# Four small transformer layers on one NeuronCore: the second layer's attention in two score orientations on 32-row tiles

## The chip, the core and the metric

The kernel runs on one core of a Trainium2 chip. The metric is device microseconds of one launch, from input in HBM to output in HBM. TensorE is PE here (its weight loads PEld), VectorE is DVE, ScalarE is ACT, GpSimd is POOL. All four work at once, each on its own list of instructions, and wait for one another by semaphores; PE writes into 8 PSUM banks of 128 partitions x 512 f32, from which ACT and DVE read.

## What is computed

x is [4, 256, 128] in f32: four batches of 256 tokens with 128 features. Four layers follow one another, all conditioned on `cond_1024` [4, 128]: an attention block with 16 heads of 64 and an MLP; the block below; a gated recurrence with rounded weights; a linear attention. The change touches only the attention of the second layer:

```python
nx = _ada_rmsnorm(x, time_emb, w_norm1, t1_w1, t1_b1, t1_w2, t1_b2)
q = (nx @ wq + bq).reshape(b, s, 16, 8)      # k and v likewise
q = q * c + _rotate_half(q) * si             # k likewise
scores = einsum('bshd,bthd->bhst', q, k) / sqrt(8)
probs = softmax(scores, axis=-1)
attn = einsum('bhst,bthd->bshd', probs, v).reshape(b, s, 128)
x = x + attn @ wo + bo
```

Per batch there are 16 heads of width 8 and scores of 256 x 256. The third layer also needs 768 parameters per batch from a chain of five small products on 4 rows (its "ada" chain: wa0, wa1, wa2, wa3, a norm, wa4), which doesn't depend on x.

## The kernel before

All 64 (batch, head) pairs n of the second layer go through one loop, written out by hand on each engine; the order of the instructions on an engine is the order of that engine's program.

**Split numbers.** q and k are kept in the format fp32r, each as a rounded part and the remainder (`high_parts` on ACT, L594, `low_parts` on DVE, L1594). A head of width 8 so takes 32 rows (high and low, twice), and four heads share a 128-row tile: `qaT` and `kaT` hold them, made by transposes on PE (L1041 to L1050).

**Prologue.** For all 8 token tiles: the QKV product (PE, L1027 to L1037), bias and rotary embedding (DVE, L1602 to L1617), high and low parts, transposes, copies into `qaT` and `kaT` (ACT, L601 to L609). PE waits for all 16 copies before the loop (L1051). As the score matmul runs over all 128 rows, the keys of a head are copied alone into a tile that is zero elsewhere (`kaM`, `masked_key`); the zeros come from a memset on POOL (L402).

**Loop** (PE L1096, ACT L655, DVE L1693). For head i:
- PE `scores` (L837): two matmuls, queries of 128 tokens against 256 keys, into bank i % 2.
- DVE `top` (L1437): the largest score of each query, negated.
- ACT `core_exp` (L501): exp with that bias, two instructions, each with an accumulator read for the sum; then the key copy of head i + 16.
- PE `turn` (L846), two heads behind: four 128 x 128 transposes of the probabilities.
- DVE `take` (L1443): copy to SBUF.
- PE `values` (L854), three heads behind: for both query tiles two f32 matmuls with 96 columns of v streamed against the turned probabilities as weights.
- DVE `normalise` (L1449), once for four heads.

**Woven in.** `weave(i)` on ACT (L626), PE (L1074) and DVE (L1640) puts one step of the ada chain behind head i, by the table `WEAVE` and the offsets USE to RESULT (L278 to L282). POOL rounds the weights of the third layer meanwhile. A Silu in this chain makes ACT load its table, and then exp's again. The outputs of the first two batches (`turn_outputs`, `outputs`, `attention_out`) stand at steps 61 to 66, those of the other two behind the loop (L1126 to L1129).

**The first attention** (L907 to L943), which the prediction reads for its prices, is not touched: `pair_scores` (L907) uses two tiles of 64 rows, `pair_values` (L935) two of 64 columns, `turn0` (L921) and `unit` (L887, L892) the full width.

## Time and profile before

| | us |
|---|---|
| median of 3 runs | 548.98 (541.31, 548.98, 555.68) |
| the profiled execution, its own time | 544.12 |
| its span, first to last instruction | 542.3 |
| PE busy in it | 416.3 |
| DVE busy | 404.0 |
| ACT busy | 307.4 |

The profiled execution takes 1.8 us more than its span. It lies between the lowest run and the median. "Busy" for PE counts from the first of several overlapping matmuls to the last one's end, each with its pipeline's latency; the time between the starts of two matmuls is what one costs in a row of them. PEclk is the clock granted to TensorE, 1.00 for 2.4 GHz and 0.50 for 1.2 GHz.

### The profile page before, as it was taken

To read this page: it belongs to the slowest core of one execution; us is meant where nothing else is said; L and a number is where in the kernel's file an instruction comes from. 1 tells how busy PE (TensorE), PEld (TensorE's weight loads), DVE (VectorE), ACT (ScalarE), POOL (GpSimd) and SP (SyncE) were. 2 spreads that over 40 slices of the span, in tenths; PEclk is the share of its full clock that TensorE was granted. 3 is DMA by queue.
4 is the path that set the end of the run, shared out by engine and by line. 5 is a ranking of instruction groups with operands and counts; after the bars stand their busy time and mean duration, and the time that the engine had idled before them with its cause. 6 is when DMAs were issued, how large, how long until landed. Compare 5 with 4: busy or idle time off the path is not lost.

```text
span 542.3 us, 8231 instructions
## 1 busy us (share of the span) xinstructions
PE 416.3 (77%) x2672; PEld 311.0 (57%) x2673; DVE 404.0 (74%) x1032; ACT 307.4 (57%) x969; POOL 128.4 (24%) x125
## 2 busy tenths in 40 slices
PE   4899999999988799666998999799992531055564
PEld 4656576576565486356897899688452421013353
DVE  4379679879799652976996888876259559979794
ACT  1564665864755424469789788555631861275252
POOL 1000000000000056400085854300663013272101
PEclk9999999999999979888999899999798555555597
DMA  8940000000000000000000000000000000000001
GB/s 311 445 152 2 1 0 2 1 1 1 2 0 1 1 2 0 0 1 0 2 2 1 2 2 0 2 1 2 0 1 1 0 0 2 0 0 1 1 0 39
DMA packets 3841, 13.32 MB, mean 25 GB/s; under 512 B 372, under 2 KB 2420, under 8 KB 3284
## 3 DMA queue, kind: packets, MB, share of 16 engines
q1 hardware_dynamic: 3800, 12.80, 6.0%
q8 instruction: 22, 0.36, 0.3%
q14 instruction: 19, 0.16, 0.1%
HBM read 12.28 MB, written 0.52 MB: 24 GB/s over the span
## 4 chain that ended last, share of the span: by engine, by line
PE 49%; DVE 28%; ACT 12%; issue 7%; POOL 2%; DMA 1%; POOLq 0%; SPq 0%; ACTq 0%; DVEq 0%
PE bank L887 6%; PE bank L864 5%; ACT big L480 4%; PE bank L907 4%; PE bank L935 4%; PE bank L921 4%; DVE area L1296 3%; ACT tab_ L480 3%; PE bank L949 3%; PE bank L892 3%; DVE area L1299 2%; DVE nmax L1440 2%; DVE tab_ L1296 2%; PE bank L1006 2%; PE bank L850 2%
## 5 line engine op out<-in xcount | busy, mean ns | idle before, releaser
L480 ACT ACTIVATE big<-bank,nmax 128x256 f32<-128x256 f32 x128 | 59.2, 473 | 29.7 <-DVE nmax L1474 16.3
L480 ACT ACTIVATE tab_<-bank,nmax 128x256 f32<-128x256 f32 x128 | 59.3, 467 | 26.9 <-DVE nmax L1440 24.8
L864 PE MATMUL bank<-vpad,xT 128*128 128x96 f32 x512 | 69.5, 280 | 5.0 <-DVE xT L1446 4.7
L864 PEld LDWEIGHTS bank<-vpad,xT 128*128 128x128 f32 x512 | 63.7, 195 | 9.1 <-DVE xT L1446 8.1
L480 ACT ACTIVATE area<-bank 128x512 f32<-128x512 f32 (+3 forms) x68 | 36.9, 550 | 53.0 <-PE bank L892 16.2
L1440 DVE TENSOR_REDUCE nmax<-bank 128x2 f32<-128x512 f32 x64 | 43.5, 679 | 10.3 <-PE bank L841 10.0
L1482 DVE COPY area<-bank 128x512 f32<-128x512 f32 x64 | 42.3, 683 | 10.2 <-PE bank L921 10.2
L396 POOL TENSOR_TENSOR rstd<-rstd,halves 128x2 f32<-128x2 f32 x4 | 2.8, 699 | 182.0 <-DVE rstd L1299 182.0
L1446 DVE COPY xT<-bank 128x512 f32<-128x512 f32 x64 | 43.4, 677 | 1.8 <-PE bank L850 1.5
L921 PE MATMUL bank<-tabs,big 128*128 128x128 f32 x256 | 37.6, 278 | 7.8 <-DVE big L1299 7.8
L921 PEld LDWEIGHTS bank<-tabs,big 128*128 128x128 f32 x256 | 29.8, 141 | 23.6 <-DVE big L1299 14.2
L1474 DVE TENSOR_REDUCE nmax<-bank 128x2 f32<-128x512 f32 x64 | 41.5, 683 | 0.4 <-PE bank L907 0.4
L850 PE MATMUL bank<-tabs,tab_ 128*128 128x128 f32 x256 | 39.8, 280 | 0.0
L1299 DVE TENSOR_SCALAR big<-big,rrec 128x256 f32<-128x256 f32 x128 | 36.5, 349 | 1.1
L887 PE MATMUL bank<-xT,w0s 128*128 128x256 f32 x128 | 33.9, 396 | 4.2 <-issue 4.2
L841 PE MATMUL bank<-kaM,qaT 128*128 128x256 f32 x128 | 31.6, 330 | 6.6 <-ACT tab_ L480 5.3
L907 PE MATMUL bank<-area 64*128 64x256 f32 x256 | 36.3, 402 | 0.0
L1165 PE MATMUL bank<-identb,area 128*128 128x128 bf16 x40 | 6.0, 310 | 38.1 <-DVE area L1299 38.0
L935 PE MATMUL bank<-area 128*64 128x256 f32 x256 | 34.7, 392 | 0.6 <-ACT big L480 0.6
L431 POOL TENSOR_SCALAR w2s<-w2s 128x768 f32<-128x768 f32 (+4 forms) x15 | 32.5, 2164 | 1.2
L480 ACT ACTIVATE big<-bank 128x256 f32<-128x256 f32 (+1 forms) x41 | 17.8, 435 | 25.0 <-PE bank L935 15.1
L850 PEld LDWEIGHTS bank<-tabs,tab_ 128*128 128x128 f32 x256 | 30.6, 144 | 0.0
(219 smaller groups left out, 888.9 us busy)
## 6 DMA issues: line engine op xcount, KB each, us to landing
w2s<-w SPq DMA_DIRECT2D x1, 4352.0 KB, 26.7
rows<-row SPq DMA_DIRECT2D x1, 1600.0 KB, 11.3
w0s<-w SPq DMA_DIRECT2D x3, 512.0 KB, 7.2
w1s<-w SPq DMA_DIRECT2D x1, 1408.0 KB, 16.2
w0s<-w SPq DMA_DIRECT2D x1, 1024.0 KB, 13.3
xs<-x SPq DMA_DIRECT2D x1, 512.0 KB, 4.6
out<-tab_ SPq DMA_DIRECT2D x2, 256.0 KB, 2.3
tabs<-tab SPq DMA_DIRECT2D x1, 421.5 KB, 5.7
```

Source lines behind the costliest of these rows:

```text
L480: return nc.scalar.activation(o, i, f, **kw)
L850: m = nc.tensor.transpose(bank[2 + half][:, k * SEQ + q * P:k * SEQ + (q + 1) * P], A.prob[:, slot, q, k * P:(k + 1) * P], ident)
L864: m = mm(bank[4 + gslot][:, o:o + v(k).shape[1]], A.pT[:, half, k, q * P:(q + 1) * P], v(k), start=(k == 0), stop=(k == QT - 1))
L887: m = mm(to[:, cc * SEQ:(cc + 1) * SEQ], part(w0s, W0, "qkv", at, at + P), rhs, start=True, stop=True)
L907: m = mm(bank[(2 * p + a) % 4][:, q * SEQ:(q + 1) * SEQ], qT[r, b % 2, c, q * P:(q + 1) * P], kT[r, b % 2, c, :], start=True, stop=True)
L921: m = nc.tensor.transpose(bank[4 + n % 2][:, k * SEQ + q * P:k * SEQ + (q + 1) * P], prob[:, n % 4, q, k * P:(k + 1) * P], ident)
L935: m = mm(bank[6][a * DH0:(a + 1) * DH0, 0:SEQ], vs[:, b % 2, k, (2 * c + a) * DH0:(2 * c + a + 1) * DH0], pT[:, n % 4, k, :], start=(k == ...
L1299: return V.tensor_scalar(o, a, s1, s2, op0, op1) if s2 is not None else V.tensor_scalar(o, a, s1, None, op0)
L1440: V.tensor_reduce(nmax[:, half, :], bank[half][:, :].rearrange("p (q k) -> p q k", q=QT), AX, ALU.max, negate=True).then_inc(S(A.tag + "_m ...
L1446: V.tensor_copy(A.pT[:, half, :, :].rearrange("p k q -> p (k q)"), bank[2 + half][:, :]).then_inc(S(A.tag + "_pT"), 1)
L1474: V.tensor_reduce(nmax0[:, n % 4, :], bank[n % 4][:, :].rearrange("p (q k) -> p q k", q=QT), AX, ALU.max, negate=True).then_inc(S("a0_max" ...
L1482: V.tensor_copy(pT[:, n % 4].rearrange("p k q -> p (k q)"), bank[4 + n % 2][:, :]).then_inc(S("a0_pT"), 1)
```

## The change

- Scores are made twice. `scores1(i)` makes queries x keys for the maxima alone: two full-width matmuls over all 128 rows of `qaT` and `kaT` (they sum over the four heads of a tile), and then, into the same places of the bank, two over only the head's 32 rows, which overwrite them. `scores_less_max(n)`, 14 heads behind, makes keys x queries on the head's 32 rows and adds the negated maxima by a second 32-row matmul with a constant selector (`msel`). `kaM` and its memset and copies are gone.
- Maxima of eight heads are split in high and low (`max_parts`), turned (`turn_max`) and copied (`take_max`).
- ACT makes one exp of 128 x 512 a head, with no bias and no sum (`exponents1`), into one of 6 buffers.
- `values1`, once for four heads: v (8 columns and a column of ones for the sum, padded to 32) is the weight, the exponents stream with 256 columns; the four heads use four 32-column tiles of bank 4. The result is copied, turned (`turn_values`) and divided (`normalise1`) by tile of 128 tokens.
- Before the loop only batch 0 is prepared; QKV, rope, high and low parts and transposes of the others stand at fixed steps of the loop (`of_batch`). Banks 5 and 6 are shared in turn by all such work (`shared_bank`, `shared_taken`). Four products of 512 columns, whose result is not used, stand before the first transposes.
- The loop has 86 steps; the ada chain has other steps, one bank (7), and its rows lie elsewhere. The table from HBM has 256 columns more.

The core of the diff (helpers for slots and views left out, as well as the ACT and DVE calls that only follow their PE partners):

```diff
-        WEAVE = {"wa0": 2, "wa1": 12, "wa2": 25, "wa3": 35, "wr": 47, "wa4": 49}
-        OUT_STEP = 61
-        USE, TOP, WORTH, SCALE, CLIP, TURN, TAKE, PRODUCT, RESULT = 1, 2, 3, 4, 5, 6, 7, 8, 9
+        WEAVE = {"wa0": 0, "wa1": 11, "wa2": 27, "wa3": 38, "wr": 52, "wa4": 55}
+        USE, TOP, WORTH, SCALE, CLIP, TURN, TAKE, PRODUCT, RESULT = 2, 3, 4, 5, 6, 7, 8, 9, 10
         NH = NB * H
-        class Core:
-            def __init__(self, tag, dh, prob, pT):
-                self.tag, self.dh, self.prob, self.pT = tag, dh, prob, pT
-        A1 = Core("a1", DH1, prob1, pT1)
+        LAG = 14
+        STEPS = NH + 22
+        MAX_PARTS, MAX_TURN, MAX_TAKE = 8, 9, 10
+        VALUES, VALUES_TAKE, OUT_TURN, OUT_TAKE = LAG + 5, LAG + 6, LAG + 19, LAG + 20
+        ATT_TURN, ATT_TAKE, ATT_OUT, ATT_ADD = 52, 53, 54, 56
...
+        QKV_STEP, ROPE_STEP, HIGH_STEP, LOW_STEP, PART_STEP = (1, 3), (2, 4), (7, 8), (8, 9), (9, 10, 11, 12)
...
+        def shared_uses():
+            uses = [("qkv", t) for t in range(QT)] + [("part", n) for n in range(4)]
+            for i in range(STEPS):
+                uses += [("max", o) for o in octet(i, MAX_TURN)]
+                uses += [("qkv", t) for t in of_batch(i, QKV_STEP)]
+                uses += [("part", n) for n in of_batch(i, PART_STEP)]
+                uses += [("out", n) for n in out_tile(i, OUT_TURN)]
+                uses += [("att", 0)] if i == ATT_TURN else []
+                uses += [("wo", 0)] if i == ATT_OUT else []
+            return uses + [("att", 1), ("wo", 1)]
+        def shared_bank(kind, n):
+            return 6 - SHARED.index((kind, n)) % 2
+        def shared_taken(kind, n):
+            use = SHARED.index((kind, n))
+            return (SHARED_TAKEN[SHARED[use - 2][0]], SHARED[use - 2][1] + 1) if use >= 2 else ("xT", 2 * NB + 2)
...
+            pool.memset(vz[:, :, :], 1.0).then_inc(S("vz_ones"), 1)
...
+            def exponents1(n):
+                act.wait_ge(S("a1_ST"), n + 1)
+                if n >= 6:
+                    act.wait_ge(S("a1_PV"), (n - 6) // 4 + 1)
+                acti(pT1[n % 6], bank[2 + n % 2][:, :], ACT.Exp).then_inc(S("a1_exp"), 1)
+            def take_max(o):
+                act.wait_ge(S("a1_mT"), o + 1)
+                acti(mT[:, o % 2, :], bank[shared_bank("max", o)][:, 0:SEQ], ACT.Copy).then_inc(S("a1_mTs"), 1)
+            def take_values(g):
+                act.wait_ge(S("a1_PV"), g + 1)
+                if g >= 4:
+                    act.wait_ge(S("a1_oT"), QT * (g // 4))
+                acti(oT[:, g % 4, :], bank[4][:, 0:SEQ], ACT.Copy).then_inc(S("a1_o"), 1)
...
+            def to_shared(kind, n):
+                sem, count = shared_taken(kind, n)
+                pe.wait_ge(S(sem), count)
+                return bank[shared_bank(kind, n)]
+            def qkv1(t):
+                pe.wait_ge(S("xT"), 2 * NB + t // QT + 1)
+                to = to_shared("qkv", t)
+                mm(to[:, 0:3 * P], xT[:, t * P:(t + 1) * P], part(w1s, W1, "qkv"), start=True, stop=True
+                   ).then_inc(S("a1_qkvmm"), 1)
+            def turn_part(n):
                 b, i, c = n // 4, n // 2 % 2, n % 2
                 pe.wait_ge(S("a1_lo"), 2 * b + i + 1)
-                if n >= 2:
-                    pe.wait_ge(S("a1_taken"), n - 1)
+                to = to_shared("part", n)
                 for g in range(2):
                     for t in range(QT):
-                        m = nc.tensor.transpose(bank[6 + n % 2][:, g * SEQ + t * P:g * SEQ + (t + 1) * P],
-                                                qka[:, b % 2, i, t, (2 * c + g) * P:(2 * c + g + 1) * P], ident)
+                        m = nc.tensor.transpose(to[:, g * SEQ + t * P:g * SEQ + (t + 1) * P],
+                                                qka[:, i, t, (2 * c + g) * P:(2 * c + g + 1) * P], ident)
                 m.then_inc(S("a1_part"), 1)
-            pe.wait_ge(S("a1_taken"), 4 * NB)
+            def scores1(n):
+                b, g, r = n // H, n % H // 4, head_rows(n)
+                pe.wait_ge(S("a1_taken"), 4 * b + 4)
+                if n < 2:
+                    pe.wait_ge(S("x_ready"), 2)
+                else:
+                    pe.wait_ge(S("a1_max"), n - 1)
+                for q in range(QT):
+                    mm(bank[n % 2][:, q * SEQ:(q + 1) * SEQ], qaT[:, g, b * SEQ + q * P:b * SEQ + (q + 1) * P],
+                       kaT[:, g, b * SEQ:(b + 1) * SEQ], start=True, stop=True)
+                for q in range(QT):
+                    m = mm(bank[n % 2][:, q * SEQ:(q + 1) * SEQ], qaT[r, g, b * SEQ + q * P:b * SEQ + (q + 1) * P],
+                           kaT[r, g, b * SEQ:(b + 1) * SEQ], start=True, stop=True)
+                m.then_inc(S("a1_S"), 1)
+            def turn_max(o):
+                pe.wait_ge(S("a1_nm"), o + 1)
+                to = to_shared("max", o)
+                for q in range(QT):
+                    m = nc.tensor.transpose(to[:, q * P:(q + 1) * P], nmx[:, q, :].bitcast(F32), ident)
+                m.then_inc(S("a1_mT"), 1)
+            def scores_less_max(n):
+                b, g, r = n // H, n % H // 4, head_rows(n)
+                pe.wait_ge(S("a1_mTs"), n // 8 + 1)
+                if n >= 2:
+                    pe.wait_ge(S("a1_exp"), n - 1)
+                for k in range(QT):
+                    to = bank[2 + n % 2][:, k * SEQ:(k + 1) * SEQ]
+                    mm(to, kaT[r, g, b * SEQ + k * P:b * SEQ + (k + 1) * P], qaT[r, g, b * SEQ:(b + 1) * SEQ],
+                       start=True, stop=False)
+                    m = mm(to, msel[r, g % 2 * P:(g % 2 + 1) * P],
+                           mT[r, n // 8 % 2, :], start=False, stop=True)
+                m.then_inc(S("a1_ST"), 1)
+            def values1(g):
+                pe.wait_ge(S("a1_exp"), 4 * g + 4)
+                if g >= 1:
+                    pe.wait_ge(S("a1_o"), g)
+                for k in range(QT):
+                    for n in range(4 * g, 4 * g + 4):
+                        at = n % H * (DH1 + 1)
+                        m = mm(bank[4][head_rows(n), 0:SEQ], vz[:, n // H * QT + k, at:at + 32],
+                               pT1[n % 6][:, k * SEQ:(k + 1) * SEQ], start=(k == 0), stop=(k == QT - 1))
+                m.then_inc(S("a1_PV"), 1)
+            def turn_values(n):
+                b, q = n // QT, n % QT
+                pe.wait_ge(S("a1_o"), 4 * b + 4)
+                to = to_shared("out", n)
+                for g in range(4):
+                    m = nc.tensor.transpose(to[:, g * P:(g + 1) * P], oT[:, g, q * P:(q + 1) * P], ident)
+                m.then_inc(S("a1_oT"), 1)
+            pe.wait_ge(S("msel"), 1)
+            for t in range(QT):
+                qkv1(t)
+            normed_T("n1a", 1)
+            pe.wait_ge(S("x_ready"), 2)
+            for u in range(4):
+                mm(bank[u % 2][:, :], part(w1s, W1, "wo"), xT[:, 0:512], start=True, stop=True)
+            for n in range(4):
+                turn_part(n)
             pe.wait_ge(S("wscale"), 1)
+            pe.wait_ge(S("xT"), 3 * NB)
...
-            for i in range(NH + 3):
+            for i in range(STEPS):
+                for o in octet(i, MAX_TURN):
+                    turn_max(o)
                 if i < NH:
-                    g, at = i % H // 4, i // H * SEQ
-                    if i < H:
-                        pe.wait_ge(S("a1_kM0"), i + 1)
-                    else:
-                        pe.wait_ge(S("a1_kM"), i - H + 1)
-                    scores(A1, i, i % 2, lambda q: qaT[:, g, at + q * P:at + (q + 1) * P], kaM[:, i % H, :])
-                if 2 <= i < NH + 2:
-                    turn(A1, i - 2, (i - 2) % 3, i % 2)
-                if i >= 3:
-                    n = i - 3
-                    values(A1, n, n % 2, (n // 4) % 2, n % 4,
-                           lambda k: vpad[:, (n // H * QT + k) * P + n % H * DH1:][:, 0:96],
-                           n // 4 if n % 4 == 0 else None)
+                    scores1(i)
+                if 0 <= i - LAG < NH:
+                    scores_less_max(i - LAG)
+                for t in of_batch(i, QKV_STEP):
+                    qkv1(t)
+                for n in of_batch(i, PART_STEP):
+                    turn_part(n)
+                for g in quad(i, VALUES):
+                    values1(g)
+                for n in out_tile(i, OUT_TURN):
+                    turn_values(n)
+                if i == ATT_TURN:
+                    turn_outputs(0)
+                if i == ATT_OUT:
+                    outputs(0)
                 weave(i)
-                if i == OUT_STEP:
-                    pe.wait_ge(S("ada_piece"), ada_pieces("wa4") + 2)
-                    turn_outputs(0)
-                if i == OUT_STEP + 3:
-                    outputs(0)
...
+            def top1(n):
+                dve.wait_ge(S("a1_S"), n + 1)
+                V.tensor_reduce(nmax[:, n // 8, :, n % 8], bank[n % 2][:, :].rearrange("p (q k) -> p q k", q=QT), AX,
+                                ALU.max, negate=True).then_inc(S("a1_max"), 1)
+            def max_parts(o):
+                dve.wait_ge(S("a1_max"), 8 * o + 8)
+                if o >= 1:
+                    dve.wait_ge(S("a1_mT"), o)
+                both = nmx[:, :, :].rearrange("p q (r h x) -> p q r h x", r=8, x=2)
+                src = nmax[:, o, :, :].unsqueeze(2).to_broadcast([P, QT, 8, 8])
+                link(V.tensor_copy(both[:, :, :, :, 0], src))
+                tt(both[:, :, :, :, 1], src, both[:, :, :, :, 0].bitcast(F32), ALU.subtract).then_inc(S("a1_nm"), 1)
+            def normalise1(n):
+                dve.wait_ge(S("a1_oT"), n + 1)
+                o = bank[shared_bank("out", n)][:, :].rearrange("p (h c) -> p h c", c=32)
+                if n >= 2:
+                    dve.wait_ge(S("a1_norm"), n - 1)
+                link(V.reciprocal(rrec[:, n % 2, :], o[:, :, DH1]))
+                tt(att1[:, n, :].rearrange("p (h d) -> p h d", d=DH1), o[:, :, 0:DH1],
+                   rrec[:, n % 2, :].unsqueeze(2).to_broadcast([P, H, DH1])).then_inc(S("a1_norm"), 1)
+            dve.wait_ge(S("vz_ones"), 1)
+            V.tensor_copy(msel[:, :], part(tabs, TAB, "msel")).then_inc(S("msel"), 1)
+            for t in range(QT):
+                take_qkv(t)
+                rope(t)
+            rms_norm("n1a", 1)
+            for m in range(2):
+                low_parts(m)
...
```

## Rows read from the trace of the kernel before

**Rows 1.** Head of the page: span, busy time, PE busy in 40 slices.
```profile
span 542.3 us, 8231 instructions
...
PE 416.3 (77%) x2672; PEld 311.0 (57%) x2673; DVE 404.0 (74%) x1032; ACT 307.4 (57%) x969; POOL 128.4 (24%) x125
...
PE   4899999999988799666998999799992531055564
```

**Rows 2.** Loop: stretch, us, busy (x) PE PEld DVE ACT POOL, PEclk, DMA, GB/s.
```profile
247.20:376.60 129.40, 118.42 (x948) 109.61 (x948) 107.77 (x244) 97.06 (x335) 50.12 (x39) 0.97 0.01 1
```

**Rows 3.** Groups by line, whole trace: count, busy us, mean ns, idle before, releaser.
```profile
L1440 DVE TENSOR_REDUCE nmax<-bank 128x2 f32<-128x512 f32 x64 | 43.5, 679 | 10.3 <-PE bank L841 10.0
...
L480 ACT ACTIVATE big<-bank,cols 128x512 f32<-128x512 f32 x8 | 5.5, 687 | 4.9 <-PE bank L1015 4.9
```

**Rows 4.** One head in order of time on PE: start us, us, engine, line.
```profile
331.03 0.51 PE L841 MATMUL bank<-kaM,qaT 128*128 128x256 f32 x2
331.37 0.60 PE L850 MATMUL bank<-tabs,tab_ 128*128 128x128 f32 x4
331.81 1.03 PE L864 MATMUL bank<-vpad,xT 128*128 128x96 f32 x8
332.77 0.32 PE L1070 MATMUL bank<-w0s,a4T 128*4 128x384 bf16 x1
333.02 0.50 PE L841 MATMUL bank<-kaM,qaT 128*128 128x256 f32 x2
```

**Rows 5.** The largest stall of the loop, in order of time.
```profile
294.04 1.28 ACT L480 ACT_TABLE_LOAD   x1
...
298.49 0.36 PE L841 MATMUL bank<-kaM,qaT 128*128 128x256 f32 x1 [2.49 <-ACT tab_ L480]
```

**Rows 6.** First attention, PE in order of time; merged rows of several windows.
```profile
56.16 0.60 PE L921 MATMUL bank<-tabs,big 128*128 128x128 f32 x4
...
58.03 0.60 PE L907 MATMUL bank<-area 64*128 64x256 f32 x4
58.03 0.81 PE L907 MATMUL bank<-area 64*128 64x256 f32 x6
...
59.31 0.59 PE L892 MATMUL bank<-w0s,xT 128*128 128x512 f32 x1
59.74 0.27 PE L921 MATMUL bank<-tabs,big 128*128 128x128 f32 x1
```

**Rows 7.** Prologue of the second attention, in order of time, and the loop's end.
```profile
219.76 2.85 PE L1034 MATMUL bank<-w1s,xT 128*128 128x384 f32 x8 [0.71 <-ACT xT L480]
...
222.58 0.28 DVE L1296 TENSOR_TENSOR vpad<-bank,rows 128x128 f32<-128x128 f32 x1
...
224.43 0.28 DVE L1299 TENSOR_SCALAR xn<-xs,area 128x128 f32<-128x128 f32 x1
...
226.66 4.54 PE L1034 MATMUL bank<-w1s,xT 128*128 128x384 f32 x8 [0.65 <-ACT xT L480]
...
228.92 1.28 DVE L1296 TENSOR_TENSOR big<-tab_,big 128x512 fp32r<-128x512 f32 x2
...
247.20 0.71 PE L841 MATMUL bank<-kaM,qaT 128*128 128x256 f32 x4 [1.20 <-DVE kaM L1626]
...
376.60 0.66 PE L1086 MATMUL bank<-tabs,xn 128*128 128x128 f32 x4 [0.62 <-DVE xn L1296]
```

**Rows 8.** POOL's memset and VectorE beside it, in order of time.
```profile
194.97 3.69 DVE L1299 TENSOR_SCALAR xn<-xs,mv,rstd 128x128 f32<-128x128 f32 x2 [0.81 <-POOL rstd L396]
195.00 3.51 POOL L402 MEMSET kaM<- 128x4096 f32 x1
```

**Rows 9.** Behind the loop: L1123 in time, then stretches as in rows 2.
```profile
380.83 2.20 PE L1123 MATMUL bank<-adrs,tabs 4*128 4x384 f32 x6
...
380.85:384.27 3.42, 3.42 (x10) 1.69 (x10) 1.04 (x2) 3.33 (x13) 0.87 (x2) 1.00 0.00 0
384.27:387.68 3.41, 3.41 (x6) 1.15 (x4) 0.94 (x4) 0.58 (x2) 3.04 (x6) 0.50 0.00 0
```

More of the change, by code:

```diff
@@ L327, in ada_pieces, with at_step, octet, quad @@
             return sum(len(splits(ADA_SHAPE[n][2])) for n in ADA_NAMES[:ADA_NAMES.index(name)])
-        def parts_of(b, i, low, dt):
-            t = qka[:, b % 2, i].rearrange("p t (h r d) -> p (t h) r d", r=4, d=DH1)
+        def at_step(i, first, every, count):
+            n = (i - first) // every
+            return [n] if i >= first and (i - first) % every == 0 and n < count else []
+        def octet(i, offset):
+            return at_step(i, offset, 8, NH // 8)
+        def quad(i, offset):
+            return at_step(i, offset, 4, NH // 4)
@@ L1928, in shape_tables @@
     t[:, slice(*at["blocks"])] = (p[:, None] // DH1 == p[None, :] // DH1)
+    msel = np.zeros((P, 2, P), np.float32)
+    for h in range(8):
+        at_row = 32 * (h % 4) + 2 * h
+        msel[at_row:at_row + 2, h // 4, :] = 1.0
+    t[:, slice(*at["msel"])] = msel.reshape(P, 2 * P)
     t[:, slice(*at["inv_n"])] = np.array([1.0 / size for _, size in QUANT], np.float32)
```

294 lines of the change are left out of this document (120 added, 174 removed).

## The prediction

> **What bounds the kernel now.** I read the page's head first [rows 1]: the span is 542.3 us, and in the quarter of it from about 247 to 377 us the PE line stands at 8 to 9 tenths. Those 129.4 us are the change's place: the loop over the 64 heads of the second attention. The table by stretches [rows 2] has PE busy 118.4 us of them, VectorE 107.8, ScalarE 97.1, at a granted clock of 0.97: TensorE sets the pace, and 129.4/64 = 2.02 us is the mean of a head. Then I read the groups of that stretch [rows 3] and one head in order of time [rows 4]: two score matmuls (L841; the second adds 0.12 us), four transposes (L850; each 0.11 us after the last), eight value instructions (L864, two for each of four f32 matmuls, eight in 1.03 us, so 0.11 apart). That is 0.24 + 0.44 + 0.88 = 1.56 us; the ada product woven in (L1070) makes the head there 331.03 to 333.02 = 2.0 us. The rest of the 129.4 us is waits: the largest lies where ScalarE loads two tables for one Silu [rows 5], after which PE had stood 2.49 us.
>
> **What the change removes.** (a) The transposes of the probabilities (4 x 0.11 us a head), their copy by VectorE (L1446, as large as the reduction of L1440), ScalarE's second exp and the accumulator reads: scores are made a second time in the other orientation, so exp's output is already what the value matmul streams. (b) 32 value instructions of 0.11 us for four heads become 16 with 256 columns. (c) Three of the four batches leave the prologue and go into the loop. VectorE's and ScalarE's savings count for little, since PE is the bound, but they decide that PE stays it: in steps 14 to 63 VectorE keeps one reduction of 0.68 us a head and some 34 us of other work (four tiles of rope 7.4, low parts 2.6, maxima 4.2, normalise 2, attention_out 1.4, ada about 16), 1.4 us a step; ScalarE has one exp of at most 0.69 us (L480, 128x512) [rows 3] and copies, near 1.2.
>
> **What a TensorE mode change costs.** This is the price that decides, and the first attention shows it [rows 6]. There PE goes from full width (L921) to 64-column tiles (L935), 64-row tiles (L907) and back to full (L892). Inside L907 two more instructions add 0.81 - 0.60 = 0.21 us, and L892's two are 59.74 - 59.31 = 0.43 us apart for 512 columns: 0.21 us is the stream of 256 f32 columns, and two tiles run in it together. From 56.16 to 59.74 us PE issued 4 transposes (0.44), 8 + 8 tiled instructions in pairs (0.84 + 0.84) and 2 of L892 (0.86): 2.98 us of stream in 3.58 us. The 0.60 us over belongs to three changes of tiling: 0.2 us each; I take 0.19. A change between full width and 32 rows isn't in the trace; its ends are 0.1 (only a weight load, the 0.11 us pitch of L850) and 0.3 us, and I take the value of the nearest row. The Trainium skill (TensorEngine Tiling (Array Packing), Key Properties) says that a change of tiling mode drains TensorE while another tile of the same mode doesn't; the 0.60 us above agrees. Without that rule's cost the change would be worth some 20 us more.
>
> **A step after the change (14 to 63), PE.** Two full-width score matmuls 0.24; change 0.19; on 32 rows two score matmuls (0.24) and the four of scores_less_max (0.48), which are on another row group (n and n - 14 differ mod 4) and so can begin beside the second of the former: 0.60 rather than 0.72 (all beside one another: 0.48); change back 0.19. Sum 1.22 us, x 50 = 61.0. The ends: a mode change of 0.1 or 0.3 us gives 9 less or 11 more; 0.48 or 0.72 gives 6 less or 6 more.
> To it come, in these 50 steps:
> - values1, 12 times: 16 instructions of 0.21 us four at a time = 0.86, plus one more mode change: 1.05 each, 12.6. The trace shows two column tiles together, not four; in pairs only, it is 10 more.
> - qkv1, 4 tiles of two instructions, 0.33 each by L1034, eight in 2.85 [rows 7]: 2.6.
> - turn_part 8 x 0.44 = 3.5; turn_max 7 x 0.22 = 1.5; turn_values 4 x 0.44 = 1.8; turn_outputs and outputs of half 0: 1.4.
> - ada: 11 products at 0.16, turns 0.7, and 10 separate visits at 0.3 for their own mode changes: 5.5. Four steps with both full-width extras and values: 0.8.
> Sum 29.7. The Silu stall stays, but exp now runs 14 steps behind the maxima and has two heads of room: 2 us. Steps 14 to 63: 61.0 + 29.7 + 2 = 92.7 us, 1.85 a step.
>
> **The ends of the loop.** Steps 0 to 13 have only scores: PE 0.24 + 0.19 + 0.24 + 0.19 = 0.86 x 14 = 12.0, plus 1.3 (qkv), 1.8 (parts), 0.8 (maxima, ada) = 15.9; VectorE 14 x 0.68 = 9.5, two tiles of take_qkv and rope at 1.85 (222.58 to 224.43) = 3.7, low parts 1.3, max_parts 0.6, ada 2 = 17.1. With two banks between the two: 18. Steps 64 to 77: PE 14 x 4 x 0.12 = 6.7, values 3.7, turns 1.5, ada 2.5 = 14.4 (ScalarE's 14 exps 9.7 lie beside it). Steps 78 to 85 are a chain: exp 0.69, values 1.05, copy, turn, normalise, second turn, normalise: 4.5. Loop: 18 + 92.7 + 14.4 + 4.5 = 129.6 us. So the 64 heads cost as much as before, with 22 steps of run-in and run-out.
>
> **The prologue.** Before, the first score is at 247.20 us [rows 7]. After: qkv for tiles 0 and 1 as now (219.8 to 222.6; the shared bank waits for the second xT piece, +0.4), rope to 224.43, plus 0.7 for the bank wait and the msel copy; then rms_norm (0.9), four transposes and two xT pieces (as in the trace, to 227.8), a high part, and low parts from 228.4 (two in 1.28); four turn_parts and copies, 0.6 each and two of each beside one another, to 232.6. The four filler products (8 x 0.43 = 3.4 us at half clock, 512 columns) fit before the low parts, or miss by up to 1 us. First score: 233. Saved: 14 us; a wait that goes is not replaced before 233, because ScalarE's Silu table load now comes 14 steps ahead of the first exp. Between 0 and 1.5 us may be lost to waits for the two shared banks behind which qkv1, turn_part and the maxima queue in order on PE.
>
> **Small edits.** POOL's memset shrinks from 4096 to 1344 columns a partition. The present one runs 195.00 to 198.51 and VectorE's L1299 beside it took 3.69 us for two [rows 8]; but PE was on L988 and L993 until 199.05 and needed the result only then: 0, at most 0.3 us. The table is 131 KB longer in a queue of 12.8 MB, at the 311 GB/s of the first slice 0.4 us ahead of the QKV weights: +0.3. The first half's output is added at step 56, and its squares no longer wait at the end: 0, since PE's own sequence (L1086, L1123, L1092) stays last there.
>
> **The sum.** Loop end 233 + 129.6 = 362.6 against 376.60 us (L1086, first instruction behind the loop): -14.0. Clock: the 32-row steps stream a quarter of the rows. At 380.85 to 384.27 PE was busy without a gap, mostly with L1123's four-row products, and the next stretch was granted 0.50, i.e. 1.2 GHz [rows 9]. So busy time alone doesn't hold 2.4 GHz. In the steady steps half of the stream is full-width work and the values fill all rows, so I expect 1.0 there and some loss in steps 4 to 8 and in the run-out: +3. Total -11 on a profiled execution of 544.1 us: 533. The median of the three runs is 549.0 (541.3 to 555.7), so the same saving from there gives 538; I forecast 533, and the range covers both. A measurement of this kernel tells about 2% (11 us) from no change: my forecast lies just beyond.
>
> **Rivals.**
> A, forecast: 523 to 543. Chance 0.56.
> B, the mode change to 32 rows costs 0.1 us and the row groups overlap fully: 9 + 6 us better, 518. For it: a 32-row tile has less to empty. Against: 64-row and 64-column changes both cost 0.2 [rows 6]. 0.14.
> C, nothing won: mode change 0.3 us, or four column tiles only in pairs (+10 or +11): 543 or 544; with both 554. For it: no row shows either. Against: the pairs of L935 and L907 are perfect. 0.12.
> D, slower: the clock. Place: the loop, PE at 1.2 GHz. Price: PE's stream of 1.22 + 0.59 a step doubles but for the mode changes, +1.45 us x 50, and +10 at either end: +92 us were it all of the loop. It decides from 15% of the loop on (14/92: nothing is left of the gain) and makes the kernel 2% slower from 27%. At 40%: +37, 567. For it: rows 9, and L1034's eight took 4.54 against 2.85 us after PE had been idle [rows 7]. Against: the loop now runs at 0.97 with 96 columns streamed per weight load, and 0.24 us of full-width stream stands in each step. 0.14.
> E, on one row group the next weight load waits for the running stream: 0.22 rather than 0.12 a matmul, +0.28 us in a steady step, +14, and +9 at the ends: 556. Against: L907's pairs follow at the bare 0.21 us, though every matmul has a load of its own (2672 matmuls, 2673 loads) [rows 1]. 0.04. The Trainium skill (TensorE: Matmul & The Clock Gate, Part 3, The mechanism) says that a weight load overlaps a running matmul only where the row groups differ, or into the background buffer; the first half of that sentence is this rival, and the 0.21 us pitch of L907 speaks for the second.
>
> **Chances.** Faster by over 2% (under 538): B, and two thirds of A: 0.53. Within 2%: a third of A, nearly all of C, half of E: 0.34. Slower: most of D and the rest of E: 0.13. Range: B with its cheapest values (512) to D at 29% of the loop (557).
>
> **What would show it.** The first score matmul near 233 us; a steady step of 1.8 to 1.9 us between VectorE's reductions, 0.9 to 1.3 in the first 14; a gap of 0.2 us between the last full-width score and the first 32-row one; granted clock over 0.93 in the loop; the loop end near 363. Wrong if: the reductions stand 1.5 us apart (B), the clock row shows 0.50 stretches in steps 14 to 63 (D), the value group of 16 takes 1.7 us (C), or VectorE has no gaps (then it, not PE, is the bound).

## The result, and the profile after

The changed kernel takes 581.12 us (median of 4 runs, 578.43 to 600.09); the kernel before, beside it on the same chip, 552.33 us (4 runs, 541.31 to 557.25). The ratio is 1.066, with a 95% interval of 1.058 to 1.073: slower by 6 to 7%, where 533 us was forecast. Some executions of either kernel run up to 4% longer at a lower granted clock (600.09 here; 548.98 to 557.25 before), and the ratios, here and below, leave them out while the medians don't. The profiled execution took 578.43 us, 45.4 more than forecast.

The head of the page after, for [rows 1]; PEclk is the granted clock in tenths, in 40 slices of 14.4 us:

```profile
span 576.6 us, 7755 instructions
...
PE 456.9 (79%) x2600; PEld 304.5 (53%) x2601; DVE 368.3 (64%) x937; ACT 267.6 (46%) x753; POOL 125.3 (22%) x124
...
PE   5899999999887975999999999997997252064574
...
PEclk9999999999999897755659998555579565555587
```

PE has fewer instructions than before (2600 against 2672) and is busy 40.6 us longer. The last line says why: the loop lies in the 17th to 28th slices, and there it reads 5 to 7 in all but four (the 22nd to 25th, at 8 and 9), where the loop before had 0.97 [rows 2]. The same by stretches, columns as in [rows 2]. The first runs from head 0's reduction to head 14's, the second to head 63's, the third to the first transposes behind the loop (they start at 401.33 us), the fourth is the start of the feed-forward; the last is a piece of the second:

```profile
240.30:266.70 26.40, 26.18 (x84) 18.56 (x84) 16.25 (x41) 6.48 (x15) 6.43 (x7) 0.52 0.00 1
266.70:366.70 100.00, 98.19 (x675) 67.41 (x674) 59.85 (x136) 48.38 (x96) 42.98 (x33) 0.77 0.01 1
366.70:401.80 35.10, 30.95 (x170) 17.93 (x170) 5.24 (x18) 12.45 (x31) 1.24 (x2) 0.50 0.00 0
401.80:421.80 20.00, 20.00 (x41) 10.01 (x40) 2.70 (x8) 7.70 (x20) 9.38 (x11) 0.50 0.01 2
319.70:357.20 37.50, 37.20 (x331) 26.86 (x331) 26.36 (x55) 22.41 (x48) 16.99 (x17) 1.00 0.00 1
```

TensorE was busy 98 to 99% of the first two stretches and still ran at 1.2 GHz through all but 0.9 us of the first and nearly half of the second. The same loop at both levels, as the group of VectorE's reductions (one a head), first in 319.7 to 357.2 us, then in 285.5 to 302.6 us, which was at 0.50 throughout:

```profile
L1687 DVE TENSOR_REDUCE nmax<-bank 128x2 f32<-128x512 f32 x23 | 15.8, 689 | 11.6 <-PE bank L1084 11.5
```

```profile
L1687 DVE TENSOR_REDUCE nmax<-bank 128x2 f32<-128x512 f32 x6 | 4.2, 692 | 8.0 <-PE bank L1084 8.0
```

37.5/23 = 1.63 us a head at 2.4 GHz, 17.1/6 = 2.85 us at 1.2 GHz; as the woven work differs between the two, both are rough. My 1.85 lies between. One bare step at 2.4 GHz in order of time, for [rows 4]:

```profile
322.52 0.50 PE L1081 MATMUL bank<-kaT,qaT 128*128 128x256 f32 x2
322.95 0.38 PE L1084 MATMUL bank<-kaT,qaT 32*128 32x256 f32 x1
322.96 0.38 PE L1104 MATMUL bank<-qaT,kaT 32*128 32x256 f32 x1
323.18 0.27 PE L1084 MATMUL bank<-kaT,qaT 32*128 32x256 f32 x1
323.18 0.28 PE L1106 MATMUL bank<-mT,msel 32*128 32x256 f32 x1
323.30 0.28 PE L1104 MATMUL bank<-qaT,kaT 32*128 32x256 f32 x1
323.42 0.27 PE L1106 MATMUL bank<-mT,msel 32*128 32x256 f32 x1
323.62 0.50 PE L1081 MATMUL bank<-kaT,qaT 128*128 128x256 f32 x2
```

The step is 1.10 us, not 1.22: L1084 and L1104 start 0.01 us apart, the second pair together, so two row groups stream wholly side by side.

### The profile page after: what moved, and what is told of

Same layout as the page of the kernel before. It is cut to its first block, busy times and chain, and to the rows that moved or that the text cites. A ratio compares the mean times of both kernels' runs of the same rounds, so it can differ in the third digit from the quotient of the medians.

```text
span 576.6 us, 7755 instructions
## 1 busy us (share of the span) xinstructions
PE 456.9 (79%) x2600; PEld 304.5 (53%) x2601; DVE 368.3 (64%) x937; ACT 267.6 (46%) x753; POOL 125.3 (22%) x124
## 4 chain that ended last, share of the span: by engine, by line
PE 63%; DVE 21%; ACT 8%; issue 5%; POOL 1%; DMA 1%; POOLq 0%; SPq 0%; ACTq 0%; DVEq 0%
PE bank L912 6%; PE bank L1084 5%; PE bank L1081 5%; PE bank L1118 4%; PE bank L932 4%; PE bank L960 4%; PE bank L946 4%; ACT big L525 4%; PE bank L974 3%; PE bank L1104 3%; PE bank L917 2%; DVE area L1386 2%; DVE area L1389 2%; PE bank L1240 2%; PE bank L1106 2%
## 5 line engine op out<-in xcount | busy, mean ns | idle before, releaser
L525 ACT ACTIVATE big<-bank 128x512 f32<-128x512 f32 (+1 forms) x84 | 43.5, 518 | 70.0 <-PE bank L1106 43.3
L525 ACT ACTIVATE area<-bank 128x512 f32<-128x512 f32 (+4 forms) x84 | 43.2, 518 | 60.2 <-PE bank L917 16.2
L1104 PE MATMUL bank<-qaT,kaT 32*128 32x256 f32 x128 | 46.8, 402 | 1.5 <-ACT big L525 0.8
L1081 PE MATMUL bank<-kaT,qaT 128*128 128x256 f32 x128 | 41.2, 412 | 1.1 <-ACT kaT L525 0.9
L1084 PE MATMUL bank<-kaT,qaT 32*128 32x256 f32 x128 | 39.8, 398 | 0.0
L1106 PE MATMUL bank<-mT,msel 32*128 32x256 f32 x128 | 39.3, 337 | 0.0
L1081 PEld LDWEIGHTS bank<-kaT,qaT 128*128 128x128 f32 x128 | 25.8, 248 | 14.1 <-issue 11.9
L1104 PEld LDWEIGHTS bank<-qaT,kaT 32*128 32x128 f32 x128 | 28.7, 238 | 6.6 <-issue 6.6
L1084 PEld LDWEIGHTS bank<-kaT,qaT 32*128 32x128 f32 x128 | 24.2, 235 | 11.1 <-issue 6.3
```

Of the source, the lines that this page charges most:

```text
L525: return nc.scalar.activation(o, i, f, **kw)
L1081: mm(bank[n % 2][:, q * SEQ:(q + 1) * SEQ], qaT[:, g, b * SEQ + q * P:b * SEQ + (q + 1) * P], kaT[:, g, b * SEQ:(b + 1) * SEQ], start=True ...
L1084: m = mm(bank[n % 2][:, q * SEQ:(q + 1) * SEQ], qaT[r, g, b * SEQ + q * P:b * SEQ + (q + 1) * P], kaT[r, g, b * SEQ:(b + 1) * SEQ], start= ...
L1104: mm(to, kaT[r, g, b * SEQ + k * P:b * SEQ + (k + 1) * P], qaT[r, g, b * SEQ:(b + 1) * SEQ], start=True, stop=False)
L1106: m = mm(to, msel[r, g % 2 * P:(g % 2 + 1) * P], mT[r, n // 8 % 2, :], start=False, stop=True)
```

## The experiments

Theory R: the clock came down because most of what TensorE streams uses 32 of its 128 rows. Rivals: L, the chip cuts the clock of an engine that is loaded too hard; M, the changes between tile shapes cost more than I took. Each run is timed beside the kernel before, whose medians were 545.9 to 552.4 us.

**All rows.** The head's rows `r` become all rows in both orientations, with the same instruction count. What is computed is then the sum over four heads, and the selector holds 0.25 to match.

```diff
-                    m = mm(bank[n % 2][...], qaT[r, g, ...], kaT[r, g, ...], start=True, stop=True)
+                    m = mm(bank[n % 2][...], qaT[:, g, ...], kaT[:, g, ...], start=True, stop=True)
...
-                    mm(to, kaT[r, g, ...], qaT[r, g, ...], start=True, stop=False)
-                    m = mm(to, msel[r, ...], mT[r, n // 8 % 2, :], start=False, stop=True)
+                    mm(to, kaT[:, g, ...], qaT[:, g, ...], start=True, stop=False)
+                    m = mm(to, msel[:, ...], mT[:, n // 8 % 2, :], start=False, stop=True)
```

> The 32-row score matmuls, both orientations and the correction, take all 128 rows of the same operands (the selection of the head is left out, and the indicator columns hold 0.25 so that the correction is still the maximum of what is computed). Same columns and same number of instructions, no change between row-tile modes among them. Theory R (the clock was granted at 1.2 GHz because most of what TensorE streamed used 32 of its 128 rows): granted clock 1.00 from the first score to the last, loop 125 to 135 us in place of 162.5, whole time 535 to 548 us. Rival L (the clock is cut because the engine is loaded too hard: it was busy 79% of the span against less before): more rows switch, the clock falls at least as far, and with the overlap of two row groups gone the time is 590 us or more. Rival M (the changes between tile shapes cost more than the 0.19 us I took): faster too, by the changes alone, but with the same granted clock as now, 0.77 in the steady stretch and 0.50 behind it: 560 to 570 us.

Measured: 534.16 us (533.53 to 540.83), 0.989 of the kernel before (0.979 to 0.999). The three stretches of the loop:

```profile
240.00:259.10 19.10, 14.95 (x88) 12.58 (x88) 16.23 (x40) 6.77 (x16) 3.22 (x6) 0.82 0.00 1
259.10:342.10 83.00, 76.43 (x669) 62.64 (x668) 62.77 (x137) 47.75 (x96) 46.35 (x34) 1.00 0.01 1
342.10:364.80 22.70, 19.20 (x175) 12.76 (x173) 4.65 (x15) 12.34 (x31) 0.97 (x2) 1.00 0.00 1
```

R had 1.00 from the first score on and 535 us at the least: the run-in stayed at 0.82, and the time is 0.8 us below. More rows switched, and the clock rose from 0.52, 0.77 and 0.50 to 0.82, 1.00 and 1.00; the loop fell from 161.5 to 124.8 us. L is out. M alone can't do it, since the clock rose. A step of this run, without changes between row-tile shapes:

```profile
319.32 0.48 PE L1081 MATMUL bank<-kaT,qaT 128*128 128x256 f32 x2
319.64 0.40 PE L1084 MATMUL bank<-kaT,qaT 128*128 128x256 f32 x2
...
320.35 0.29 PE L1128 MATMUL bank<-tabs,area 128*128 128x128 f32 x1
```

Eight full-width score instructions take 1.03 us here, against 1.10 us with 32-row tiles. At one clock the tiles save nothing: what the overlap gives, the two changes of shape take.

**Without the passes; passes twice.** The overwritten full-width passes (L1081) are left out, or run for `q in 2 * list(range(QT))`.

> The two full-width passes in front of each head's scores are left out (their results were overwritten). Theory R: granted clock 0.50 through the whole loop, the stretch that had 1.00 (319.7 to 357.2 us) too. The run-in gains 0.7 us per head (14 heads, 10 us), the rest pays: a steady step of 1.8 to 2.1 us at 1.2 GHz, so 570 to 590 us, near no difference from the changed kernel. Rival L: less load, the clock comes back to 1.00 and the time is below 550 us. Rival M: one change of shape and 0.42 us less per head at the same clocks: 550 to 560 us.

> The full-width passes run twice (four instead of two matmuls of 256 columns per head). Theory R: granted clock 1.00 in most of the steady stretch (steps 14 to 63) and perhaps in the run-in; there two more full-width matmuls cost 0.21 us per head (64 heads: 14 us) and the clock gives back 25 to 35 us; the run-out (steps 64 on, no passes there) stays at 0.50: 560 to 572 us. Rival L: more load, lower clock, 0.43 us more per head at 1.2 GHz: 605 us or more. Rival M: 0.21 to 0.43 us more per head at the same clocks: 595 to 608 us.

Measured without passes: 573.88 us (565.78 to 576.51). The steady stretch:

```profile
261.10:364.50 103.40, 97.34 (x574) 62.56 (x575) 62.38 (x137) 47.92 (x97) 45.33 (x34) 0.52 0.00 1
```

Less work, hardly less time: 103.4 us for the 49 steps from reduction to reduction, 2.1 us a head at 0.52, the upper end of what R gave. Passes twice: 565.75 us (563.51 to 566.82), 15 us less than the changed kernel with 128 more matmuls:

```profile
272.40:374.40 102.00, 99.83 (x773) 73.64 (x772) 62.41 (x136) 48.53 (x96) 43.17 (x33) 0.88 0.01 1
374.40:401.30 26.90, 22.46 (x172) 13.57 (x170) 4.93 (x16) 12.39 (x31) 1.23 (x2) 0.75 0.00 1
```

Both ways R's total held and those of L and M didn't. With passes twice it held by luck, though: R had 1.00 in most of the steady stretch, 25 to 35 us given back there, and the run-out still at 0.50; they were 0.88, nothing (102.0 against 100.0 us) and 0.75. The passes hold some clock, and cost nearly what they give in the steady stretch itself; the gain is behind it, where the run-out is entered at 2.4 GHz (26.9 against 35.1 us).

**Passes in the run-out.** In front of the second orientation of heads 50 to 63:

```diff
+                for u in range(1 * QT if n >= NH - LAG else 0):
+                    k = u % QT
+                    mm(bank[2 + n % 2][:, k * SEQ:(k + 1) * SEQ], kaT[:, g, ...], qaT[:, g, ...],
+                       start=True, stop=True)
```

> Two overwritten full-width passes in front of the second-orientation scores of heads 50 to 63 alone, the steps in which no first-orientation passes are left. Theory R: the granted clock of the run-out (366.7 to 401.8 us, now 0.50) comes back to 1.00 for most of it and stays for the feed-forward behind it (388 to 422 us, now 0.50): 8 to 13 us off the run-out and 5 to 10 us off the stretch behind, 558 to 570 us. Rivals L and M: 14 heads with 0.43 us more each at 1.2 GHz, part of it beside the exponents: 583 to 588 us.

Measured: 596.88 us (581.57 to 600.48). All four are above R's range, and the shortest is among those of the changed kernel, so neither gain nor loss can be told. The profiled execution is the longest one:

```profile
267.00:385.30 118.30, 117.02 (x675) 80.56 (x674) 62.30 (x136) 48.45 (x96) 42.90 (x33) 0.62 0.00 1
385.30:424.00 38.70, 36.83 (x198) 23.08 (x198) 5.09 (x17) 12.77 (x31) 1.23 (x2) 0.63 0.00 1
```

The steady stretch has the same 675 matmuls as the changed kernel's and took 118.3 us at 0.62, not 100.0 at 0.77. Both are single executions, and the changed kernel's own spread just as far (578 to 600), so this difference isn't the edit's. The run-out itself got 0.63 for 0.50 and, with the passes in it, was 3.6 us longer. So R's expectation failed here: two passes a head brought 2.4 GHz back for about a quarter of the run-out and not behind it, and nothing was won.

**Filler away.** The four products of 512 columns ahead of the loop are left out.

> The four overwritten products of 512 columns ahead of the loop are left out. They ran from 230.6 to 235.5 us at 1.2 GHz, and the first transposes of the loop's operands waited for them: without them the first score comes 3 to 5 us earlier. If they do what the clock needs there, it is at 0.50 from the first score on (it had 1.00 for the first 1.9 us), which costs at most 2 us: 576 to 583 us, no difference that can be told. If the clock at the start decides how the whole run-in and the steady stretch go, the time rises to 590 us or more.

Measured: 578.76 us (575.90 to 581.91), no difference. The first score came at 240.75 us in an execution that reached the selector's copy (the instruction on which the QKV products wait) 2.98 us later, so 1.55 us earlier by that mark, not 3 to 5: PE then stood 2.40 us ahead of the transposes. The trace calls it "issue", but the first low part, for which `turn_part` waits, ends only then:

```profile
235.26 0.69 DVE L1384 TENSOR_TENSOR big<-tab_,big 128x512 fp32r<-128x512 f32 x1 [2.32 <-ACT big L525]
236.06 3.81 PE L1068 MATMUL bank<-tabs,big 128*128 128x128 f32 x16 [2.40 <-issue]
```

The filler had held the transposes back by 2.8 us (low part done at 233.14, transposes at 235.91) and given 1.3 of them back: from there to the first score it is 3.41 us at 1.00 with it and 4.69 us at 0.54 without.

**The same edit on the kernel before.** Its score matmuls take 32 rows; the other rows of its masked keys are zero.

```diff
-                    scores(A1, i, i % 2, lambda q: qaT[:, g, ...], kaM[:, i % H, :])
+                    scores(A1, i, i % 2, lambda q: qaT[32 * (i % 4):32 * (i % 4) + 32, g, ...],
+                           kaM[32 * (i % 4):32 * (i % 4) + 32, i % H, :])
```

> The kernel before, with one thing changed: its score matmuls take the head's 32 rows of queries and of the masked keys in place of all 128 (the other rows of the keys are zero, so the result is the same). Copies, order and every other engine's work stay. Theory R: fewer rows, lower clock: the granted clock of its loop (0.97) falls to 0.5 to 0.8, and with 118 us of TensorE work in 129 us the loop grows by 25 us or more: 570 to 620 us. Rival M: two changes between shapes per head, 64 x 0.4 us, at an unchanged clock: 560 to 575 us. Rival N (rows have nothing to do with it): 541 to 556 us, clock 0.95 or more.

Measured: 641.53 us (639.74 to 641.64), 1.180 of the kernel before (1.174 to 1.185). The stretch of [rows 2], same bounds:

```profile
247.20:376.60 129.40, 125.23 (x523) 109.23 (x522) 66.74 (x144) 64.65 (x211) 38.22 (x26) 0.51 0.00 1
```

In 129.4 us it did 523 matmuls where the kernel before did 948, at 0.51 for 0.97. No instruction was added, 128 of the loop's matmuls only lost three quarters of their rows, and 95 us came of it, more than R's 570 to 620 too. M's 560 to 575 and N's 541 to 556 are both out. The products are the same, as the other rows of the keys held zeros, so it isn't the values that bring the clock down. Two things of this run go against R as worded above. Only 2 of a head's 14 matmuls are narrow, so it needn't be most of the stream:

```profile
310.00 1.11 PE L850 MATMUL bank<-tabs,tab_ 128*128 128x128 f32 x4
310.91 1.86 PE L864 MATMUL bank<-vpad,xT 128*128 128x96 f32 x8
312.70 0.79 PE L841 MATMUL bank<-kaM,qaT 32*128 32x256 f32 x2
```

And two changes of shape a head came with them, which this run can't tell from the rows (see "What stays open").

**Full rows in the useful work.** First masked keys in the first orientation alone (one part of the change undone), then in both, where each head also has a selector that is zero outside its rows (`mselM`). The copies are ScalarE's for the first, four heads ahead, and VectorE's for the second, three ahead:

```diff
-                for q in range(QT):
-                    mm(bank[n % 2][...], qaT[:, g, ...], kaT[:, g, ...], start=True, stop=True)
...
-                    m = mm(bank[n % 2][...], qaT[r, g, ...], kaT[r, g, ...], start=True, stop=True)
+                    m = mm(bank[n % 2][...], qaT[:, g, ...], kaM[:, n % 4, :], start=True, stop=True)
...
-                    mm(to, kaT[r, g, ...], qaT[r, g, ...], start=True, stop=False)
-                    m = mm(to, msel[r, ...], mT[r, n // 8 % 2, :], start=False, stop=True)
+                    mm(to, ring[n % 4][:, k * P:(k + 1) * P], qaT[:, g, ...], start=True, stop=False)
+                    m = mm(to, mselM[n % 8], mT[:, n // 8 % 2, :], start=False, stop=True)
```

> One part of the change undone: the first orientation is taken with masked keys on 128 rows (four buffers, 64 copies on ScalarE) in place of the passes and the 32-row tiles; the second orientation stays on 32-row tiles. Theory R: the run-in is no longer bound by TensorE at either clock (0.43 us per head at 1.2 GHz against 0.7 us of VectorE): 10 to 14 us in place of 26.4. The steady stretch has two matmuls and one change of shape less per head; as many full rows as before, so it has either clock in parts: 85 to 105 us. Run-out as in the changed kernel, 0.50 and 35 us: 545 to 568 us. Rival M (changes between shapes are what costs, not the clock): the loop falls by 64 x 0.6 us, 540 us or less, at a granted clock no higher than the changed kernel's.

> Full rows without wrong results: keys with zeros outside the head's 32 rows, in four buffers for the first orientation (64 copies on ScalarE) and four for the second (64 copies on VectorE), and an indicator for each head that is zero outside its rows; the overwritten passes go. The third weight block is loaded in two parts, the later one after the loop. All score matmuls stream 128 rows. Theory R (few-row streaming brought the clock down): granted clock 1.00 from step 14 to 63 and in most of the run-out; run-in bound by VectorE's maxima at 0.7 us per head (10 to 12 us, whatever the clock there), steady steps by VectorE (62.8 us of it in the all-rows run, and 50 copies of 0.28 us: 77 to 84 us), run-out 20 to 26 us: 515 to 530 us. Rival C (it was the overwritten passes that held the clock in the all-rows run, and without them 128-row scores aren't enough): the clock falls in the run-in and stays at 0.50 in the steady stretch, 555 us or more.

> As the all-rows run (every score matmul on 128 rows without the selection of the head, 0.25 in the indicator columns), and the overwritten passes left out too. Theory R: rows held the clock there, not the passes: granted clock 1.00 from step 14 on; run-in 10 to 12 us (19.1 with passes), steady stretch 83.0 less 50 x 0.21 us = 72 us, run-out 22.7: 512 to 520 us. Rival C (the passes are needed as well): clock 0.50 through the run-in and for long after it, 545 us or more.

Masked keys in the first orientation only: 600.64 us (594.98 to 604.60), above the 545 to 568 expected. In the profiled execution, of 604.10 us, the steady stretch was at 1.2 GHz nearly throughout:

```profile
262.50:393.80 131.30, 129.25 (x574) 88.35 (x572) 62.01 (x138) 70.84 (x145) 48.07 (x35) 0.54 0.00 1
```

Against the run without passes, at nearly its clock, it is 27.9 us longer (0.57 us a head); the medians are 26.8 us apart. The full-width pair no longer runs beside the second orientation, and there are two changes of shape a head again; that these two make the 0.57 us is argued, not measured. A few full rows between narrow ones pay for the change and don't keep the clock: R had it "in parts" and missed.

All rows without passes: 521.61 us (520.01 to 526.75), 0.966 (0.949 to 0.982), 1.6 us above R's range. The steady stretch:

```profile
259.50:335.70 76.20, 67.25 (x571) 52.14 (x571) 61.73 (x138) 47.29 (x97) 47.21 (x34) 0.98 0.01 1
```

So the full rows held the clock, not the passes; C is out. Masked in both: 546.10 us (median of 10, 540.64 to 553.98), 1.000 (0.995 to 1.006). The clock is as R said, the time is not:

```profile
260.40:352.90 92.50, 69.50 (x569) 52.44 (x568) 79.33 (x187) 67.70 (x143) 47.19 (x34) 0.96 0.00 1
```

VectorE and ScalarE have 17.6 and 20.4 us more work than in the run above, and VectorE is now the busiest engine (79.3 of 92.5 us). Its copies took 0.28 us in the median but 0.98 at worst, from 318.71 us, beside GpSimd's L489 (0.91 us from 318.64); beside its L491 another took 0.27. The Trainium skill (SBUF — State Buffer, SBUF: two separate sides) says that GpSimd and some kinds of VectorE instructions lock a shared port pair against each other for a whole instruction: the first copy looks so, the second doesn't.

**Keys by DMA.** The 128 copies become DMAs of 32 rows x 1 KB (`key_to`) in SyncE's queue, idle in the loop:

```diff
+            for i in range(NH + 10):
+                if i + 4 < NH:
+                    sp.wait_ge(S("a1_S"), i + 1)
+                    key_to(kaM[:, i % 4, :], i + 4, 0) 
+                n = i - 10
+                if 4 <= n < NH:
+                    sp.wait_ge(S("a1_ST"), n - 3)
+                    key_to(ring[n % 4], n, 1)
```

> The masked kernel with all 128 key copies as DMAs issued by SyncE (32 rows of 1 KB each, four buffers per orientation), so that neither ScalarE nor VectorE copies. Theory V (what the masked kernel lost against the all-rows run without passes, 546 against 522 us, is its copies: 17 us of casts on VectorE in the steady stretch, stretched by GpSimd beside them, and 19 us on ScalarE): run-in 18 to 22 us, steady stretch 76 to 82 us (92.5 with the copies, 76.2 without any), granted clock 0.95 or more there: 520 to 530 us. Rival Q (the landing of a transfer, 2 us or more, paces the heads: four buffers and a chain of score, issue, landing): run-in of 0.9 us or more per head or steady steps of 1.8 us or more, 540 us or more.

Measured: 526.42 us (520.41 to 533.35), 0.965 of the kernel before (0.959 to 0.972): faster than both kernels. The loop:

```profile
243.00:262.30 19.30, 14.88 (x59) 11.09 (x60) 15.90 (x41) 7.61 (x17) 3.29 (x6) 0.65 0.14 33
262.30:337.90 75.60, 67.21 (x572) 51.60 (x571) 61.23 (x138) 47.51 (x97) 47.10 (x34) 1.00 0.18 43
337.90:360.20 22.30, 18.79 (x171) 12.36 (x169) 4.63 (x15) 12.33 (x31) 0.60 (x2) 1.00 0.12 29
```

The DMAs land in 1.8 us in the median:

```profile
kaM<-kaT SPq DMA_DIRECT2D x64, 32.0 KB, 1.8
over<-kaT SPq DMA_DIRECT2D x64, 32.0 KB, 1.8
```

The steady stretch is as short as without any copies (75.6 against 76.2), with four buffers of lead. V held but for these 75.6 us, where it had 76 at the least. Q didn't hold: 75.6/49 is 1.5 us a step, not 1.8, and the time is under 540. (Its 0.9 us a head in the run-in told nothing, as V's own 18 us are more.) Where the landing does show is the first score:

```profile
242.52 0.47 PE L1126 MATMUL bank<-kaM,qaT 128*128 128x256 f32 x2 [2.32 <-DMA kaM<-kaT]
```

## Why the prediction was wrong, point by point

| stretch | forecast | after | all rows | keys by DMA |
|---|---|---|---|---|
| first score at | 233 | 239.3 | 239.3 | 242.5 |
| steps 0 to 13 | 18 | 26.4 (0.52) | 19.1 (0.82) | 19.3 (0.65) |
| steps 14 to 63 | 92.7 | 100.0 (0.77) | 83.0 (1.00) | 75.6 (1.00) |
| steps 64 to 85 | 18.9 | 34.6 (0.50) | 22.3 (1.00) | 22.3 (1.00) |
| behind the loop | 167.4, and 3 for the clock | 177.1 | 169.6 | 165.8 |

(us, granted clock in brackets; measured steps count from reduction to reduction, so that step 63 falls to the last ones; the last line is the execution's own time less the start of the first transposes behind the loop. The forecast's 3 us for the clock are the "+3" of "The sum", which meant them for the loop.) The differences of the forecast to after, 6.3, 8.4, 7.3, 15.7 and 6.7, and 1.0 from the first score to the first reduction, which I hadn't counted, make the 45.4 us.

**The step that failed** is in "The sum": "In the steady steps half of the stream is full-width work and the values fill all rows, so I expect 1.0 there and some loss in steps 4 to 8 and in the run-out: +3". I had the right row in hand [rows 9], a busy engine that streams few rows and loses the clock, and let one argument of a share of full-width work outweigh it. Within the loop about 105 of 161 us were at 1.2 GHz, and the 20 us behind it too. With every score matmul on 128 rows, and the same number of instructions, the loop took 124.8 us instead of 161.5: this is what the "+3" left out. That is rival D, at 0.14: at 40% of the loop's work it gave 567, and with the 6.3 of the prologue and the loss behind the loop one is at what was measured. That it comes out so well is partly luck: 105 us at 2.85 us a head and 56 at 1.63 are 37 and 34 heads' worth, so about half of the work was at 1.2 GHz, and steps cheaper than my 1.85 made up for it. D should have been the forecast, or at least have carried the range past 557.

**Right: the prices at 2.4 GHz.** A change of shape at 0.19 us: from the second L1081 (322.75) to the first L1084 are 0.20 us and from there to the second 0.23, where the all-rows run has 0.12 and 0.11 (319.52, 319.64, 319.75), so 0.08 + 0.12 = 0.20 a change. The overlap of row groups was better than taken (B's half), and all four column tiles of the values run together: two pairs of them start 0.01 us apart, and the next two 0.24 us on. In all, 1.63 us a head over 319.7 to 357.2 us where I had 1.85. The Trainium skill's rule that tiles on different row groups run at once (TensorE: Matmul & The Clock Gate, Part 3, The mechanism) agrees with the 0.01 us between L1084 and L1104; E, which came from the same page, is refuted by the pair on one row group (L1106 at 323.18, L1104 at 323.30, 0.12 us).

```profile
324.73 0.41 PE L1118 MATMUL bank<-big,area 128*32 128x256 f32 x2
324.74 0.41 PE L1118 MATMUL bank<-tab_,area 128*32 128x256 f32 x2
324.97 0.39 PE L1118 MATMUL bank<-big,area 128*32 128x256 f32 x2
```

**Wrong in size: the first score.** 6.3 us late. This execution was 2.4 us behind before the prologue began. PE then stood 2.29 us for the selector's copy, and was at 0.50 to 0.57 after it: with both, the low parts came another 1.7 us late. And the filler, which I had set before the low parts, ran behind the second half's transposes, where PE would have been free to go on from 233.14 us. I had its products at 0.43 us "at half clock"; that was the price at 2.4 GHz, and here the first four took 0.85 us each:

```profile
223.73 2.60 PE L1059 MATMUL bank<-w1s,xT 128*128 128x384 f32 x4 [2.29 <-DVE msel L1711]
229.72 1.12 PE L889 MATMUL bank<-tabs,xn 128*128 128x128 f32 x4 [3.40 <-DVE xn L1389]
230.63 5.45 PE L1137 MATMUL bank<-xT,w1s 128*128 128x512 f32 x8
235.91 1.04 PE L1068 MATMUL bank<-tabs,big 128*128 128x128 f32 x8
```

By the run without it, the filler costs 1.55 us of the 6.3. The saving of the prologue was there all the same: 247.20 against 239.3.

**Wrong in size: the run-out.** Even at 2.4 GHz the last steps take 22.3 us, not 18.9. About 1.7 of these 3.4 us are step 63 (83.0/49), which my sum has in the stretch before; the other 1.7 are missing from it, whatever the clock.

**Rivals.** A and B fall by the clock, C by 1.63 us a head at 2.4 GHz. (The 0.53 for "faster" is 0.51 by its own parts.) The sign of D's evidence was in the profile before; nothing in it gave the point at which D sets in, and that I should have kept as an open cost.

**What stays open.** First, which property of 32-row work brings the clock down. Counted in the traces, where some records are missing, over the stretches shown above (the values' 32-column tiles are a shape of their own):

| run | matmuls on 32 rows | changes of shape a us | clock |
|---|---|---|---|
| before | 0 of 933 | 0 | 0.97 |
| before, 32 rows | 75 of 499 | 0.5 | 0.51 |
| masked first only | 193 of 566 | 0.9 | 0.54 |
| passes twice | 294 of 765 | 1.1 | 0.88 |
| after | 295 of 673 | 1.1 | 0.77 |
| without passes | 293 of 574 | 0.8 | 0.52 |
| all rows | 0 of 667 | 0.3 | 1.00 |
| keys by DMA | 0 of 567 | 0.3 | 1.00 |

Without 32-row matmuls the clock is up, with them it is down at least in part; but neither their share nor the number of changes puts the runs in order. Changes alone can't be it: the run without passes has fewer than the changed kernel and a lower clock. The share alone can't be it either: of the runs below 0.9, the kernel before on 32 rows has the smallest one and the lowest clock. Nor is it any use of part of the array: the first attention's pairs of 64-row and 64-column tiles ran at 1.00 in the kernel before [rows 6]:

```profile
56.16:59.74 3.58, 3.58 (x24) 1.97 (x23) 2.49 (x7) 1.84 (x6) 0.00 (x0) 1.00 0.00 0
```

Open too is why one and the same program up to step 63 was at 0.77 in one execution and at 0.62 in another. That keys by DMA work in the kernel before was not tried.

## What to carry to other kernels

Matmuls on 32 of 128 rows are no cheaper in TensorE's time at one clock (1.10 against 1.03 us for a step here), and they can halve the clock for everything around them: taking three quarters of the rows away from 128 matmuls cost the old kernel 95 us. Keep the narrow operand in a tile that is zero elsewhere, let an idle DMA queue fill it, and read the granted clock by stretches before reading any sum of instruction times. When a row of the profile shows a busy engine at half clock, treat "does my loop look like that row" as the first question, with the full price.

## What of the hardware was not expected

- TensorE at 98 to 99% busy was granted 0.52 and 0.77 (26.4 and 100 us). The Trainium skill (TensorE: Matmul & The Clock Gate, Part 1, What's actually happening) has the clock follow how busy the engine has been; by that rule alone the loop would have run at 2.4 GHz, and the sum would have been my forecast. The runs don't agree with it: with equal instruction counts, the rows (and the changes of shape that go with them) moved the clock from 0.77 to 1.00, and in the kernel before from 0.97 to 0.51.
- Overwritten work can shorten a kernel: 128 more matmuls, 15 us less. It is a poor way all the same; full rows in the useful work gave 0.965 of the kernel before, passes twice 1.043.
- The same instructions can be granted either level: the run-out was at 0.50 where it was entered at 1.2 GHz (after), and at 0.75 with passes twice, where it was entered at 2.4 GHz. These are one profiled execution each. It is no latch: in the changed kernel's loop the clock came back to 1.00 for 319.7 to 357.2 us, amid the same mix of work.
